# Decay attention: scores kept in SBUF and issued a step ahead, and the transposed rows of the second head copied by VectorE

## The reference, cut to what matters

```python
q, k, v = (proj(q_w, q_b), proj(k_w, k_b), proj(v_w, v_b))
scores = jnp.einsum('bhqd,bhkd->bhqk', q, k) / jnp.sqrt(jnp.float32(dk))
p_ = jax.nn.softmax(jnp.where(mask, scores, -1e+32), axis=-1) * mask
distcum = jnp.cumsum(p_, axis=-1)
disttotal = p_.sum(-1, keepdims=True)
dist = stop_gradient(jnp.sqrt(jnp.clip((disttotal - distcum) * pos, 0.0)))
total_effect = jnp.clip(jnp.exp(dist * gamma), 1e-05, 100000.0)
scores = jnp.where(mask, scores * total_effect, -1e+32)
p = jax.nn.softmax(scores, axis=-1)
out = jnp.einsum('bhqk,bhkd->bhqd', p, v)
```

## Time and profile before

| what | value |
|---|---|
| median of 3 runs | 3239.71 us (3229.29 to 3274.91) |
| the profiled execution, its own time | 3245.55 us |
| its span, first to last instruction | 3243.8 us |
| PE, DVE, ACT, POOL busy over the span | 2771.9, 1960.9, 1513.2, 1261.0 us |
| decay attention, first to last scan (128 steps) | 1827.5 to 3023.6 us |
| mean granted PE clock, whole span | 0.848 |

### The profile page before, as it was taken

The page is one execution under the profiler, slowest core; times in us unless marked ns, Lnnn a source line. Parts: engine busy times, 40 slices in busy tenths (PEclk is TensorE's granted clock), DMA queues, the critical chain, the costliest instruction groups (busy, mean ns, idle before and its releaser), DMA issues. The chain is left out here.

```text
span 3243.8 us, 60046 instructions
## 1 busy us (share of the span) xinstructions
PE 2771.9 (85%) x21812; PEld 1904.3 (59%) x21812; DVE 1960.9 (60%) x3888; ACT 1513.2 (47%) x2961; POOL 1261.0 (39%) x1551
## 2 busy tenths in 40 slices
PE   7998699992999999999997687888888888888476
PEld 6887477772555555555554465565555555555365
DVE  4995477775444454444444567666776677676624
...
GB/s 42 39 41 4 7 2 2 2 2 24 1 1 0 0 0 0 0 0 0 0 0 21 1 1 2 1 1 1 2 1 1 1 2 1 1 2 1 4 1 53
DMA packets 31576, 21.60 MB, mean 7 GB/s; under 512 B 24553, under 2 KB 28649, under 8 KB 31364
## 3 DMA queue, kind: packets, MB, share of 16 engines
...
## 5 line engine op out<-in xcount | busy, mean ns | idle before, releaser
L1245 DVE TENSOR_TENSOR prod<-c_h,act 128x512 f32<-128x512 f32 x352 | 243.4, 692 | 481.0 <-PE c_h L1097 439.0
L1177 ACT ACTIVATE act<-c_h 128x512 f32<-128x512 f32 x352 | 210.2, 597 | 655.9 <-PE c_h L1097 655.9
L1428 POOL TENSOR_TENSOR d_decay<-d_later,d_posg 128x768 f32<-128x768 f32 x128 | 232.6, 1817 | 437.5 <-DVE d_later L1827 437.5
L1124 PE MATMUL c_out<-e_w,hid 128*128 128x64 f32 x2816 | 388.7, 281 | 0.1
L1124 PEld LDWEIGHTS c_out<-e_w,hid 128*128 128x128 f32 x2816 | 340.6, 191 | 79.5 <-issue 79.3
L1071 POOL TENSOR_TENSOR x_rest<-flatT,x_hm 64x512 f32<-64x512 bf16 (+1 forms) x33 | 38.2, 1156 | 748.8 <-ACT x_hm L1157 724.8
L1469 PE MATMUL d_T<-ident,d_p 128*128 128x128 f32 x768 | 165.7, 336 | 184.2 <-ACT d_pT L1603 104.5
L1827 DVE TENSOR_TENSOR_SCAN d_later<-d_cont,d_ex 128x768 f32<-128x768 f32 x128 | 225.1, 1759 | 73.8 <-ACT d_ex L1621 73.8
L1097 PE MATMUL c_h<-x_hm,e_w_hh 128*128 128x512 bf16 x704 | 267.5, 380 | 0.9 <-ACT wT L1170 0.9
L1097 PE MATMUL c_h<-x_hm,e_w_mm 128*128 128x512 bf16 x704 | 267.6, 380 | 0.0
L1097 PE MATMUL c_h<-x_hl,e_w_lh 128*128 128x512 bf16 x704 | 267.4, 380 | 0.0
...
## 6 DMA issues: line engine op xcount, KB each, us to landing
...
rows<-in_table,idx POOLq DMA_INDIRECT x128
...
```

The lines of the kernel that those rows point to most:

```text
L1124: last = nc.tensor.matmul(bo[:, b * D:(b + 1) * D], hid[u][:, b * P:(b + 1) * P], w2[:, c, :], start=(c == 0 and b == 0), stop=(c == NCH - ...
L1177: nc.scalar.activation(act1[u][:], b1[u][:], ACT.Silu).then_inc(S["activated"], 1)
L1245: nc.vector.tensor_tensor(prod[u][:], b3[u][:], act1[u][:], ALU.mult).then_inc(S["multiplied"], 1)
L1428: pool.tensor_tensor(decay[u][:], later[u][:, 0:2 * SEG].rearrange("p (e s) -> p e s", e=2), posg[:, h:h + 2, :], ALU.mult).then_inc(U["pl ...
```

## The change

- The scores of pair K+1 are issued in PE's step K, ahead of the turns, and no longer wait for `weighed` but for `S_kept` of the pair two before.
- ACT gets a new copy d_kept <- d_S (128 x 768) in step K for pair K+1. DVE's max, shift and weighing read d_kept in SBUF (4 buffers) in the place of d_S in PSUM.
- On DVE the weighing with its maxima moves from step K+1, behind the scan, to step K+2, ahead of the scan. The copy of head 1's turned rows moves from ACT to DVE; in DVE's list it stands behind shift (and d_y), ahead of the weighing.
- On ACT the order of a step changes: copy of head 0's turned rows, exp, Ln, Exp, the q copy (j = 0), d_attT, the new copy, the third Exp, the other copies and statistics, and as its last the second exp, which stood in the middle before.
- On POOL placed moves from the end of step K to the beginning of step K+1, and shift2 from the beginning to the end of its step.
- The fillers: 3 (not 4) behind the scores, 3 behind head 0's turn, 3 behind head 1's turn in even steps, 3 behind the turn back in odd steps. That makes 9 a step, 4 before.

The diff, without the new tile's and semaphore's declarations:

```diff
@@ -1374,17 +1375,17 @@
                     m, j = K // PAIRS, K % PAIRS
                     if step_there(K - 1):
                         u = (K - 1) % 2
+                        h = 2 * ((K - 1) % PAIRS)
+                        pool.wait_ge(U["scanned"], K)
+                        if K - 1 >= 2:
+                            pool.wait_ge(U["weighed"], K - 2)
+                        pool.tensor_tensor(decay[u][:], later[u][:, 0:2 * SEG].rearrange("p (e s) -> p e s", e=2),
+                                           posg[:, h:h + 2, :], ALU.mult).then_inc(U["placed"], 1)
                         pool.wait_ge(U["inv_total"], 2 * K)
                         pool.wait_ge(U["placed"], K)
                         pool.tensor_tensor(long(decay[u]), long(decay[u]), wide(rtot[u], 1, P), ALU.mult)
                         pool.tensor_tensor(short(decay[u]), short(decay[u]), wide(rtot[u], 0, HALF), ALU.mult)\
                             .then_inc(U["scaled"], 1)
-                    if step_there(K - 2):
-                        u, w = (K - 2) % 2, (K - 2) % KEEP_P
-                        pool.wait_ge(U["max2_made"], 2 * (K - 1))
-                        pool.tensor_tensor(long(p2[w]), long(p2[w]), wide(mx2[u], 1, P), ALU.subtract)
-                        pool.tensor_tensor(short(p2[w]), short(p2[w]), wide(mx2[u], 0, HALF), ALU.subtract)\
-                            .then_inc(U["shifted2"], 1)
                     if j == 0:
                         n = m + 1
                         if there(n):
@@ -1419,14 +1420,12 @@
                             after(pool, "x_turned", n - 1)
                             pool.wait_ge(G["centred"], n + 1)
                             pool.tensor_tensor(xn[:], hc[:], over(rstd[:], D), ALU.mult).then_inc(G["xn_made"], 1)
-                    if step_there(K):
-                        u = K % 2
-                        h = 2 * j
-                        pool.wait_ge(U["scanned"], K + 1)
-                        if K >= 2:
-                            pool.wait_ge(U["weighed"], K - 1)
-                        pool.tensor_tensor(decay[u][:], later[u][:, 0:2 * SEG].rearrange("p (e s) -> p e s", e=2),
-                                           posg[:, h:h + 2, :], ALU.mult).then_inc(U["placed"], 1)
+                    if step_there(K - 2):
+                        u, w = K % 2, (K - 2) % KEEP_P
+                        pool.wait_ge(U["max2_made"], 2 * (K - 1))
+                        pool.tensor_tensor(long(p2[w]), long(p2[w]), wide(mx2[u], 1, P), ALU.subtract)
+                        pool.tensor_tensor(short(p2[w]), short(p2[w]), wide(mx2[u], 0, HALF), ALU.subtract)\
+                            .then_inc(U["shifted2"], 1)
 
             @block.tensor
             def _(pe):
@@ -1445,7 +1444,7 @@
                         pe.wait_ge(G["q_kept"], 2 * (m + 1))
                         pe.wait_ge(G["k_kept"], m + 1)
                     if K >= 2:
-                        pe.wait_ge(U["weighed"], K - 1)
+                        pe.wait_ge(U["S_kept"], K - 1)
                     for e in range(2):
                         nc.tensor.matmul(bS[u][:, e, 0:SEG], ident_b[:], hide[:], start=True, stop=False)
                     for g, S in ((0, 1), (1, 1), (0, 0), (1, 0)):
@@ -1497,6 +1496,10 @@
                     pe.wait_ge(Q["near_done"], i + 1)
                     weigh_values(1, 0).then_inc(Q["attended"], 1)
 
+                def keep_warm():
+                    for _ in range(WARM):
+                        nc.tensor.matmul(bO[:], ident_b[:], fill[:], start=True, stop=True)
+
                 def turn_pairs(bank, at, tile, made):
                     for g in range(2):
                         last = nc.tensor.transpose(bank[:, at + g * P:at + (g + 1) * P],
@@ -1514,14 +1517,15 @@
                 for K in range(FIRST, LAST + 1):
                     m, j = K // PAIRS, K % PAIRS
                     i = (K - 5) // 2
+                    if step_there(K + 1):
+                        scores(K + 1)
                     if step_there(K):
-                        scores(K)
                         if quad_there((K - 6) // 2):
                             pe.wait_ge(Q["attT_kept"], (K - 6) // 2 + 1)
-                        for _ in range(WARM):
-                            nc.tensor.matmul(bO[:], ident_b[:], fill[:], start=True, stop=True)
+                        keep_warm()
                     if step_there(K - 3):
                         turn(K - 3, 0)
+                        keep_warm()
                     if j == 0:
                         if there(m + 1):
                             pe.wait_ge(G["hT_kept"], m + 2)
@@ -1548,6 +1552,8 @@
                         values(i)
                     if step_there(K - 3):
                         turn(K - 3, 1)
+                        if K % 2 == 0:
+                            keep_warm()
                     if j == 1 and there(m + 1):
                         pe.wait_ge(G["hTr_kept"], m + 2)
                         after(pe, "zb_made", m + 2)
@@ -1595,8 +1602,8 @@
                 nc.scalar.activation(gab[:], gab[:], ACT.Ln, bias=1.0).then_inc(softened, 1)
                 act.wait_ge(ready, READY)
 
-                def keep_turned(K, e):
-                    w = 2 * K + e
+                def keep_turned(K):
+                    w = 2 * K
                     act.wait_ge(U["turned"], w + 1)
                     if w >= KEEP_T:
                         act.wait_ge(Q["attended"], (w - KEEP_T) // QUAD + 1)
@@ -1610,25 +1617,17 @@
                 for K in range(FIRST, LAST + 1):
                     m, j = K // PAIRS, K % PAIRS
                     i = (K - 5) // 2
+                    if step_there(K - 3):
+                        keep_turned(K - 3)
+                    if step_there(K):
+                        act.wait_ge(U["shifted"], 2 * (K + 1))
+                        nc.scalar.activation(ex[K % 2][:], ex[K % 2][:], ACT.Exp).then_inc(U["exped"], 1)
                     if step_there(K - 1):
                         u = (K - 1) % 2
                         act.wait_ge(U["scaled"], K)
                         nc.scalar.activation(decay[u][:], decay[u][:], ACT.Ln, bias=1e-18).then_inc(U["log_done"], 1)
                         act.wait_ge(U["log_done"], K)
                         nc.scalar.activation(decay[u][:], decay[u][:], ACT.Exp, scale=0.5).then_inc(U["root_done"], 1)
-                    if step_there(K):
-                        act.wait_ge(U["shifted"], 2 * (K + 1))
-                        nc.scalar.activation(ex[K % 2][:], ex[K % 2][:], ACT.Exp).then_inc(U["exped"], 1)
-                    if step_there(K - 1):
-                        u = (K - 1) % 2
-                        act.wait_ge(U["root_done"], K)
-                        nc.scalar.activation(decay[u][:], decay[u][:], ACT.Exp, scale=-1.0).then_inc(U["decay_made"], 1)
-                    if step_there(K - 3):
-                        keep_turned(K - 3, 0)
-                    if step_there(K - 2):
-                        w = (K - 2) % KEEP_P
-                        act.wait_ge(U["shifted2"], K - 1)
-                        nc.scalar.activation(p2[w][:], p2[w][:], ACT.Exp).then_inc(U["exped2"], 1)
                     if j == 0:
                         n = m + 1
                         if there(n):
@@ -1649,8 +1648,16 @@
                         if i >= 1:
                             act.wait_ge(Q["back"], i)
                         nc.scalar.activation(attT[:], bO[:], ACT.Copy).then_inc(Q["attT_kept"], 1)
-                    if step_there(K - 3):
-                        keep_turned(K - 3, 1)
+                    if step_there(K + 1):
+                        act.wait_ge(U["scored"], K + 2)
+                        if K + 1 >= KEEP_S:
+                            act.wait_ge(U["weighed"], K + 2 - KEEP_S)
+                        nc.scalar.activation(kept[(K + 1) % KEEP_S][:], bS[(K + 1) % 2][:, :, 0:SEG], ACT.Copy)\
+                            .then_inc(U["S_kept"], 1)
+                    if step_there(K - 1):
+                        u = (K - 1) % 2
+                        act.wait_ge(U["root_done"], K)
+                        nc.scalar.activation(decay[u][:], decay[u][:], ACT.Exp, scale=-1.0).then_inc(U["decay_made"], 1)
                     if j == 0:
                         n = m + 2
                         if there(n):
@@ -1703,6 +1710,10 @@
                             after(act, "q_made", n - 1)
                             after(act, "hTr_kept", n - 1)
                             nc.scalar.activation(hT[:], X0[:, 2 * P:4 * P], ACT.Copy).then_inc(G["hT_kept"], 1)
+                    if step_there(K - 2):
+                        w = (K - 2) % KEEP_P
+                        act.wait_ge(U["shifted2"], K - 1)
+                        nc.scalar.activation(p2[w][:], p2[w][:], ACT.Exp).then_inc(U["exped2"], 1)
 
             @block.vector
             def _(dve):
@@ -1782,18 +1793,16 @@
                     m, j = K // PAIRS, K % PAIRS
```

(42 more changed lines are left out.)

7 lines of the change are left out of this document (4 added, 3 removed).

## The result

The changed kernel takes 3727.06 us (median of 4 runs, 3721.91 to 3739.77) where the one before takes 3234.5 (3225.95 to 3274.91): a ratio of 1.1539, 95% interval 1.1491 to 1.1587. It is 15% slower. The profiled execution took 3739.77 us, with a span of 3737.9.

What follows compares the result with a forecast made beforehand. The prediction took each step as a round trip of waits, with no engine full. Ring 10.2, lock 0.9 and clock 1.3 made 12.4 us a step against 9.42, giving 3620, forecast as 3615 us; range 3380 to 3770.

Steps and rivals of the forecast that it cites:

- The ring: DVE's copy waits for PE's turn of head 1, delaying DVE's queued work every step; 10.2 us a step at full clock.
- the stretch: PE's work from first turn's start to second turn's end; 5.45 us for j = 0, 2.66 for j = 2, 3.0 odd.
- Full clock and lock: Rival: fillers hold PE's clock full while DVE and POOL share SBUF ports; 11.15 us a step, 3467 us, chance 0.20.
- The lock in shift: DVE's shift, now with two SBUF inputs, waits behind the end of POOL's shift2; 0.3 to 0.4 us a step.
- the weighing's wait: DVE's weighing, now with two SBUF inputs, waits behind POOL's scaled in the shorter steps; 0.3 us.
- The lock in shift2: POOL's shift2 comes ready as DVE's scan begins and waits for its end; +1.6 us for j = 3, +0.4 for j = 1.
- The clock: PE's granted clock stays as it is, half the time low, lengthening the work between turns; 1.3 us a step.
- full-low price of 2.6: Cost in us a step, at most, if PE ran at 1.2 GHz all the time; the forecast charged half.
- the clock mostly low: Rival: PE's clock is mostly low as its gaps get longer; 13.3 us a step, 3742 us, chance 0.10.
- the longer gap: PE's idle time before the turn, some 3 us where 1.7 stood; given as reason for a mostly low clock.
- Fillers can't raise the clock with the gap there: Nine fillers for four on PE raise the granted clock only if gaps let them; PE's idle before d_y remains.
- The other side: Rival: head 1's turned rows are ready before DVE asks, leaving busy time; near 7.5 us a step, 3000 us, chance 0.07.

Runs made afterwards that it cites:

- e1: Changed kernel with DVE's copy of head 1's turned rows moved behind the scan and reciprocals; 3262.59 us, ratio 1.0071 to the kernel before.
- e4: Kernel before with only DVE's copy of head 1's turned rows added, ahead of the scan, in place of ACT's; 3568.81 us, ratio 1.1043.
- e6: Changed kernel with PE's work between the two turns moved behind head 1's turn; 3359.21 us, ratio 1.0407 to the kernel before.
- e9: Changed kernel with 15 fillers behind the scores in place of 3; 3507.37 us, ratio 1.0843 to the kernel before.
- e5: Changed kernel with DVE's copy behind the scan and reciprocals, and shift reading scores from PSUM; 3071.11 us, ratio 0.9522 to the kernel before.

## Why the prediction was right

I forecast 3615 us, range 3380 to 3770; 3727 was measured. Direction, ring and the presence of the lock were right; the size was 112 us short, 0.8 us of a 13.2 us step. By its own steps:

- *The ring* (10.2 us a step at full clock without lock, the copy's wait above 250 us). It is shown three times: the copy away from DVE's front gives back 464 us (e1), the copy alone makes the kernel before 10% slower (e4), and emptying the stretch shortens each kind of step by what was taken out (e6). The wait is 498.8 us in 111 steps.
- *Full clock and lock, 11.15 us.* e9 has this state: clock 0.99, 11.31 us. That the total fits is in part luck, as errors of its parts cancel. Counted from scan to scan, d_zb falls into j = 1 and the two operations of j = 3 fall into j = 0, and with the lock the terms said 13.7, 10.7, 10.3 and 10.0 for j = 0 to 3; e9 has 15.18, 10.13, 11.02 and 9.48. The even steps were too short by 1.5 and 0.7 us, the odd ones too long by 0.6 and 0.5. No run shows the 10.2 without the lock by itself.
- *The lock in shift, 0.3 to 0.4 us in every step: too small in even steps, nothing in odd ones.* I had shift wait once, behind the end of shift2. In fact DVE and POOL alternate. For j = 1 above, the long part waits for placed, then POOL's scaled goes in between the two parts, and the short part waits for it (2742.10 to 2745.63); for j = 2 and 3 the long part passes in 0.85 and the short one waits for placed. That is 2.0 us a step in DVE's durations. From the scan to the turn the terms had 5.4 us for j = 0 and 4.6 for j = 2 without lock, and it is 7.35 and 6.35: 2.0 and 1.8 us on the ring in even steps, none in odd ones. That is 0.9 us a step in the mean, 0.6 more than I had; part of that was hidden by terms that were too long, the stretch of j = 2 (2.16 in e9, 2.66 in the sum) and the weighing's wait.
- *The lock in shift2, +1.6 us for j = 3 and 0.4 for j = 1:* the instruction pays 1.38 (2.42 for 1.04) in each step; it is on the way in odd steps alone. The terms put their turn some 4.1 us behind the scan, and it is 4.08. The *weighing's* wait behind scaled, 0.3: none in the changed kernel (0.95 in every step from 20 to 110), as DVE comes to it after the stretch, when POOL is done; it appears as soon as the ring goes (1.21 in e1).
- *The clock, 1.3 us a step: this is the mis-sized term that the total shows.* "I take the clock as it is, half the time low" charged the ring with the stage's mean. The stage's mean was well forecast (0.72), but it counts PE's gaps too, with 0.99 in the one above, while the stretches have 0.60 (j = 0) and 0.50 (j = 1). It isn't only the gap right ahead: at 2757.68 (j = 2) PE has waited just 0.41 us for d_y, its granted clock has been 0.50 since the stretch before, and the turn takes 0.88. Measured 1.9 of my full-low price of 2.6, 0.6 of the 0.8 us that the forecast lacks. The rival "the clock mostly low", 3742, which I gave 0.10, was 15 us off where the forecast was 112, and I had its reason, the longer gap, in hand.
- *Fillers can't raise the clock with the gap there:* right in the main. Nine give 0.72 where four give 0.66, and the kernel with nine is the slower one. Twelve more in the gap itself do raise it (e9).
- *The other side,* turned rows ready before DVE asks, 3000 us, was rightly ruled out for this order, and is what e5 makes true: 3071.
- Of what the profile should show, j = 2 "near 10" was wrong (12.8), and so was the weighing "far above 0.92" (one of 128 took 1.36, all others 0.95). The copy's wait for j = 0, "nearly 5 us", is 8.3 in the mean; in e9, at the full clock, it is 5.6.

On the Trainium skill's rule of the shared port pair ("SBUF — State Buffer", section "SBUF: two separate sides"): the traces agree, with one operand of 128 x 4 broadcast too (shift's short part takes 1.25 to 2.04 us for 0.41 with both inputs in SBUF, and 0.41 with one in PSUM), and add that with work queued on both sides the two engines take turns by single instructions. Not all of an instruction is held up: shift2 ends 0.83 us behind the scan's end, where it takes 1.04 alone.
